# Moving the FP8 rounding of 24 tiles from the end of the attention to its middle, in a decoder block on one Trainium2 core

## The reference

```python
x = x + attention(layernorm(x))          # 32 query heads, 8 KV heads of 64, RoPE, causal, batches of 512 tokens
x = x + cross(layernorm(x), ctx)         # x, ctx: (4, 512, 512) float32
x = x + moe(layernorm(x))                # 8 experts, top 1, capacity 256, and a shared expert; hidden 704

def cross(x, weight):                    # "quantized" to float8_e4m3 and back
    xq = qdq(x, blocks of 1 x 128)       # safe = max(amax, 1e-4); round(x * 448/safe) to fp8; * safe/448
    wq = qdq(weight, blocks of 128x128)  # the same with one amax per 128 x 128 block, least 1e-6
    return einsum('emk,enk->emn', xq, wq)
```

## Time and profile before

| what | value |
| --- | --- |
| median of 3 runs | 1612.63 us (1609.43 to 1612.71) |
| the profiled execution: its own time | 1614.8 us |
| the profiled execution: its span, first to last instruction | 1613.0 us |
| mean granted TensorE clock in it | 0.956 of full speed |
| busy in the span: PE, DVE, ACT, POOL | 1467.1, 1237.6, 917.9, 1058.6 us |

### The profile page before, as it was taken

One profiled execution on the slowest core, in us unless ns is written; L12 is line 12 of the kernel. 1 busy time (PEld: TensorE's weight loads), 2 busy tenths in 40 slices (PEclk: granted clock), 3 DMA queues, 4 the chain that ended last, 5 costly groups with the idle time before them and its releaser, 6 DMA issues.

```text
span 1613.0 us, 26858 instructions
## 1 busy us (share of the span) xinstructions
PE 1467.1 (91%) x8616; PEld 1290.2 (80%) x8616; DVE 1237.6 (77%) x2986; ACT 917.9 (57%) x2277; POOL 1058.6 (66%) x1040
## 2 busy tenths in 40 slices
PE   5899999999989999999999967728889898899997
PEld 4688888888878888888888856627778787899996
DVE  6787787788887787788787879858797964677785
ACT  2587777777667777777777655422121213566562
POOL 1798888888776888888888767626252522444545
PEclk9899999999999999999999988969989899899998
DMA  5322232222312222232322333031101003577767
GB/s 189 87 73 66 81 76 71 77 81 55 81 50 63 75 74 66 81 89 55 82 76 59 112 119 92 8 125 41 52 27 53 7 27 113 160 234 221 226 209 239
DMA packets 78796, 152.13 MB, mean 94 GB/s; under 512 B 15366, under 2 KB 15622, under 8 KB 78656
## 3 DMA queue, kind: packets, MB, share of 16 engines
q1 hardware_dynamic: 76096, 142.16, 30.3%
q0 software_dynamic: 2560, 8.25, 1.5%
HBM read 87.58 MB, written 16.78 MB: 65 GB/s over the span
## 4 chain that ended last, share of the span: by engine, by line
PE 74%; DVE 12%; issue 6%; POOL 4%; ACT 2%; DMA 1%; SPq 1%; DVEq 0%; POOLq 0%; ACTq 0%
PE bank L400 15%; PE bank L401 15%; PE bank L402 15%; PE bank L442 7%; PE bank L418 5%; PE bank L457 5%; PE bank L458 5%; PE bank L419 4%; PE bank L392 2%; DVE work L943 1%; POOL P L1390 1%; DVE work L1056 1%; DVE aam L1095 1%; PE bank L429 1%; DVE st L938 1%
## 5 line engine op out<-in xcount | busy, mean ns | idle before, releaser
L742 ACT ACTIVATE P<-P,mn 128x512 f32<-128x512 f32 (+3 forms) x512 | 284.5, 556 | 221.6 <-DVE mn L994 220.9
L1390 POOL TENSOR_TENSOR P<-P,ri 128x128 f32<-128x128 f32 (+3 forms) x512 | 353.9, 724 | 10.4 <-DVE ri L983 10.4
L994 DVE CUSTOM_DVE_ANT_0 P<-bank,mask 128x512 f32<-128x512 f32 (+3 forms) x512 | 235.6, 479 | 118.3 <-PE bank L419 117.9
L1035 DVE TENSOR_TENSOR PTl<-bank,PTh 128x512 fp32r<-128x512 f32 (+1 forms) x384 | 229.2, 598 | 37.0 <-ACT PTh L754 33.9
L442 PE MATMUL bank<-ident,P 128*128 128x128 f32 x1280 | 203.4, 274 | 7.2 <-POOL P L1390 7.2
L754 ACT ACTIVATE PTh<-bank 128x512 fp32r<-128x512 f32 (+1 forms) x384 | 197.6, 516 | 6.0 <-PE bank L442 2.9
L418 PE MATMUL bank<-KT,QT 128*128 128x256 f32 (+2 forms) x512 | 191.2, 373 | 7.4 <-DVE mn L994 7.3
L457 PE MATMUL bank<-PTh,VS 128*128 128x256 f32 (+2 forms) x512 | 164.5, 332 | 11.5 <-DVE PTl L1035 8.8
L400 PE MATMUL bank<-XT,Wh 128*128 128x512 f32 x384 | 165.4, 431 | 9.6 <-DVE qcs L1007 4.7
L419 PE MATMUL bank<-KT,QT 128*128 128x256 f32 (+2 forms) x512 | 167.3, 327 | 0.0
L1428 POOL TENSOR_TENSOR OTl<-Opair,OTh 128x512 fp32r<-128x512 f32 x64 | 83.5, 1305 | 120.8 <-ACT OTh L764 120.5
(11 more groups left out here) (190 smaller groups left out, 4214.5 us busy)
## 6 DMA issues: line engine op xcount, KB each, us to landing
RW<-in_wf SPq DMA_DIRECT2D x170, 256.0 KB, 3.2
QT<-qh SPq DMA_DIRECT2D x256, 64.0 KB, 2.0
QT<-ql SPq DMA_DIRECT2D x256, 64.0 KB, 2.0
Wraw<-in_wqkv SPq DMA_DIRECT2D x16, 768.0 KB, 4.8
Oraw<-in_wo SPq DMA_DIRECT2D x16, 512.0 KB, 3.4
KT<-KT SPq DMA_DIRECT2D x32, 256.0 KB, 2.9
work<-in_ctx SPq DMA_DIRECT2D x32, 256.0 KB, 2.7
krot<-kvs SPq DMA_DIRECT2D x64, 64.0 KB, 2.0
```

The costliest lines, as they stand in the source:

```text
L742: e.activation(pq, pq, ACT.Exp, bias=mn[:, z, qb:qb + 1], scale=-1.0, accum_out=rs[:, z, qb:qb + 1]).then_inc(a_exp, 1)
L994: e.tensor_tensor_reduce(P[:, z, off[qb]:off[qb] + k], bank[n % 2][:, 0:k], mask[:, 512 - k:512], -0.125, BIG, ALU.add, ALU.min, mn[:, z, ...
L1035: e.tensor_tensor(pt_part(PTl, part), bank[2 + part][:, 0:128 * n].rearrange("p (m n) -> p m n", n=128), pt_part(PTh, part).bitcast(F32), ...
L1390: e.tensor_tensor(pq, pq, ri[:, z, qb:qb + 1].to_broadcast([128, n]), ALU.mult).then_inc(g_norm, 1)
```

## The change

Of the 32 tiles 24 are now rounded in the middle of the attention: the 16 context tiles and the 8 tiles of X that belong to batches 0 and 1. The rounded tiles are written to a new tensor `kept` in DRAM, and are loaded from there when the cross attention needs them. The buffers are `xnx` (two tiles, used otherwise for the first norms) and a new `Zb` (two tiles) for the steps.

* The 16 context tiles are loaded in steps -4 to 17 for their maxima (steps 3 to 18 on DVE). One all-reduce over all 16 tiles, in step 20, takes the place of four. The context tiles are loaded again for the rounding.
* `background()` gives the step in which each of the 24 roundings begins: 22, 25, ... 46 for tiles 0 to 8 and 61, 64, ... 103 for tiles 9 to 23. In that step SP loads the tile (or, for a tile of X, DVE makes it with its scales: `tile_scales`); one step later ACT scales it (`scaled`, four instructions of 128 columns); two steps later DVE makes the steps (`steps_of`, two instructions) and POOL adds, subtracts and scales back (`background_rounded`, three instructions, the last of them with the scale broadcast over the whole tile); four steps later SP stores it (`keep`).
* The statistics of the tiles of batches 0 and 1 are taken in steps 72 to 79.
* The zeroing of the dispatch tensor (16 transfers) moves from steps 116 to 123 to steps -3 to 4, from the new `Zb`.
* At the end of the attention the context tiles and the tiles of X of batches 0 and 1 are only loaded (`load_cw`, `load_t1`) and transposed. Batches 2 and 3 of X are rounded where they were, by the same `rounded`.

```diff
@@ slots @@
         for i in range(TB):
-            plan(s - 13 + i if b else s - 3 + i // 2, "stats2", b, i)
+            if b >= 2:
+                plan(s - 13 + i, "stats2", b, i)
+                plan(s - 1 + i, "cross_round", b, i)
             plan(s + 1 + i, "cross_turn", b, i)
             plan(s + 2 + i, "cross_product", b, i)
-            plan(s - 1 + i, "cross_round", b, i)
...
-            plan(s + i // 2, "context_max", b, i)
-        plan(s + 2, "context_all", b)
-        plan(s + 3, "context_scales", b)
-        for i in range(TB):
-            at = s + 4 + i + i // 3
-            plan(at, "context_round", b, i)
-            plan(at + 2, "context_turn", b, i)
+            plan(s + 6 + i + i // 3, "context_turn", b, i)
...
+def background():
+    return [22 + 3 * j if j < 9 else 34 + 3 * j for j in range(NBG)]
@@ scalar_engine @@
+            def scaled(j):
+                y = xnx[:, j % 2, :]
+                if j < NCTX:
+                    need.wait_ge(v_cscale, 1)
+                    need.wait_ge(d_by[j % 2], 16 * (j // 2 + 9))
+                else:
+                    need.wait_ge(v_bscale, j - NCTX + 1)
+                for c in range(4):
+                    k = wsc[:, 1, 4 * j + c:4 * j + c + 1] if j < NCTX else asc[:, j % 4, 0, c:c + 1]
+                    last = e.activation(y[:, tokens(c)], y[:, tokens(c)], ACT.Copy, scale=k)
+                last.then_inc(a_scaled, 1)
...
                     pair(h - 3)
+                if h - 1 in begins:
+                    scaled(begins[h - 1])
@@ vector_engine @@
                 if t >= 2 * TB:
                     need.wait_ge(p_xt, t - 1)
+                    need.wait_ge(d_keep, 16 * 9)
...
+            def tile_scales(j):
+                t = j - NCTX
+                y = xnx[:, j % 2, :]
+                need.wait_ge(d_keep, 16 * (j - 1))
+                after()
+                chain(normed(y, t))
+                after()
+                chain(e.tensor_reduce(aam[:, j % 4, :], four(y), AX.X, ALU.max, apply_absolute_value=True))
+                after()
+                scales(aam[:, j % 4, :], asc[:, j % 4, 0, :], asc[:, j % 4, 1, :], 1e-4).then_inc(v_bscale, 1)
+
+            def steps_of(j):
+                y, q = xnx[:, j % 2, :], Zb[:, j % 2, :]
+                need.wait_ge(a_scaled, j + 1)
...
+                chain(e.tensor_scalar(q.bitcast(U32), y.bitcast(U32), 0x7F800000, None, ALU.bitwise_and))
+                after()
+                e.tensor_scalar(q, q, 2.0 ** -6, 1.5 * 2.0 ** 20, ALU.max, ALU.mult).then_inc(v_bq, 1)
...
                     rotate(unit, 1, 1)
+                if 3 <= h < 3 + NCTX:
+                    context_max(h - 3)
+                if h == 21:
+                    context_scales()
+                if 72 <= h < 72 + 2 * TB:
+                    need.wait_ge(v_x, last_x(h - 72) + 1)
+                    stats_of(h - 72)
+                if h == 72 + 2 * TB - 1:
+                    rstd_of(slice(0, 2 * TB))
+                if begins.get(h, 0) >= NCTX:
+                    tile_scales(begins[h])
+                if h - 2 in begins:
+                    steps_of(begins[h - 2])
...
                 if 0 <= h < NH:
                     masked(h, 0)
@@ gpsimd_engine @@
+            def background_rounded(j):
+                y, q = xnx[:, j % 2, :], Zb[:, j % 2, :]
+                need.wait_ge(v_bq, j + 1)
+                e.tensor_tensor(y, y, q, ALU.add).then_inc(g_badd, 1)
+                need.wait_ge(g_badd, j + 1)
+                e.tensor_tensor(y, y, q, ALU.subtract).then_inc(g_bq, 1)
+                need.wait_ge(g_bq, j + 1)
+                d = wsc[:, 0, 4 * j:4 * j + 4] if j < NCTX else asc[:, j % 4, 1, :]
+                e.tensor_tensor(four(y), four(y), d.unsqueeze(2).to_broadcast([128, 4, 128]), ALU.mult).then_inc(g_kept, 1)
...
                     rotate(unit)
+                if h == 20:
+                    need.wait_ge(v_cmax, NCTX)
+                    e.partition_all_reduce(wsc[:, 0, :], wam[:, :, :].rearrange("p i c -> p (i c)"), 128,
+                                           bass.bass_isa.ReduceOp.max).then_inc(g_call, 1)
+                if h - 2 in begins:
+                    background_rounded(begins[h - 2])
@@ sync_engine @@
+            def keep(j):
+                need.wait_ge(g_kept, j + 1)
+                if j >= 1:
+                    need.wait_ge(d_keep, 16 * j)
+                e.dma_start(keptv[j], xnx[:, j % 2, :]).then_inc(d_keep, 16)
...
+            def load_t1(t):
+                need.wait_ge(d_keep, 16 * NBG)
+                if t < 3:
+                    need.wait_ge(p_kv, NU)
+                else:
+                    need.wait_ge(p_turn, turn_at["cross_turn", (t - 3) // TB, (t - 3) % TB] + 1)
+                e.dma_start(T1[t % 3], keptv[NCTX + t]).then_inc(d_t1[t % 3], 16)
...
+                if h in (-4, -3):
+                    load_background(h + 4)
+                if 3 < h < 2 + NCTX:
+                    load_background(h - 2)
+                if h - 4 in begins:
+                    keep(begins[h - 4])
+                if begins.get(h, NCTX) < NCTX:
+                    load_background(NCTX + begins[h])
```

More of the change, by code:

```diff
@@ L15 @@
 CHUNK_BANK = (4, 5, 7)
+NCTX, NBG = 16, 24
 class Once:
@@ L173, in decoder @@
         xd = nc.dram_tensor("xd", (NE * CAP, D), F32).ap()
+        kept = nc.dram_tensor("kept", (NBG * 128, D), F32).ap()
         oe = nc.dram_tensor("oe", (NE * CAP, D), F32).ap()
@@ L183, in decoder @@
         d_cw = [sem(f"d_cw{i}") for i in range(3)]
+        d_t1 = [sem(f"d_t1{i}") for i in range(3)]
+        d_by = [sem(f"d_by{i}") for i in range(2)]
+        d_keep = sem("d_keep")
         d_xe = [sem(f"d_xe{i}") for i in range(2)]
@@ L214, in decoder @@
         NCT = 4
-        rounds = [x for x in in_order if x[0] in ("context_round", "cross_round")]
+        rounds = [x for x in in_order if x[0] == "cross_round"]
+        begins = {at: j for j, at in enumerate(background())}
         round_at = {x: n for n, x in enumerate(rounds)}
@@ L524, in turn @@
                     need.wait_ge(v_turn, n - 1)
+                t = b * TB + i
                 if stage == "context_turn":
-                    need.wait_ge(g_q, round_at["context_round", b, i] + 1)
+                    need.wait_ge(d_cw[t % 3], 16 * (t // 3 + 1))
+                elif stage == "cross_turn" and b < 2:
+                    need.wait_ge(d_t1[t % 3], 16 * (t // 3 + 1))
                 elif stage == "cross_turn":
@@ L1631, in side_slot @@
                     stage, b, i = x
-                    if stage == "context_max":
-                        load_cw(b, *((3, 0) if i == 0 else (i - 1, 1)))
-                    elif stage == "context_turn":
-                        if i == 0:
-                            load_cw(b, 3, 1)
-                        elif b + 1 < NB:
-                            load_cw(b + 1, i - 1, 0)
+                    t = b * TB + i
+                    if stage == "context_turn" and t + 3 < NCTX:
+                        load_cw(t + 3)
+                    elif stage == "cross_turn" and t + 3 < 2 * TB:
+                        load_t1(t + 3)
                     elif stage == "load_x":
@@ L1676, in sync_engine @@
                     side_slot(h - NH - 15)
-                if h == NH - 14:
-                    for i in range(3):
-                        load_cw(0, i, 0)
-                if NH - 12 <= h < NH - 4:
+                if h in (-4, -3):
[6 more added lines that the diff above has]
+                    load_background(NCTX + begins[h])
+                if -3 <= h < 5:
                     for i in range(2):
                         need.wait_ge(g_zero, 1)
-                        e.dma_start(xdz[2 * (h - NH + 12) + i], T1[0]).then_inc(d_zero, 16)
+                        e.dma_start(xdz[2 * (h + 3) + i], Zb[:, 0, :]).then_inc(d_zero, 16)
+                if h == NH - 14:
+                    for t in range(3):
+                        load_cw(t)
+                if h == NH - 8:
+                    for t in range(3):
+                        load_t1(t)
                 if h == NH - 6:
```

97 lines of the change are left out of this document (42 added, 55 removed).

## The result

The changed kernel takes 1657.83 us (median of 4 runs, 1653.38 to 1665.72) against 1612.04 before: ratio 1.029, 95% interval 1.025 to 1.033. The forecast was 1596, faster than before, its range 1562 to 1624. The profiled execution took 1658.05 us with a span of 1656.2, 43.2 more than before.

The account below looks back on a forecast made before the run. The prediction took PE to bound the kernel except where the attention ends and the MoE begins. From a 1613.0 us span, minus 66 saved plus 50 of costs gave 1597, a median of about 1596 us, likeliest range 1582 to 1608.

Parts of the forecast that it names:

- The two sums: Whole kernel: 66 us saved at the attention's end and behind it, 50 us of costs added, mostly in the attention.
- The tail: Steps 120 to 134 and behind the attention: removed roundings, all-reduces and waits save 66 us.
- The all-reduce: Step 20, on POOL ahead of head 20's `normalised`: PE stalls for 10 us, plus 4 for the clock, 14.
- POOL: In the attention: three instructions per tile, 3.7 us, delay `normalised` and stall PE by 18 us over 72 heads.
- the slack of that is the end of POOL's four instructions to PE's L442: In the attention: room before POOL's lateness stalls PE's transposes, 0.9 to 6.3 us over eight heads.
- PE waiting for L1390's successor: In the attention: PE should wait for this POOL output ahead of the transposes of heads 0, 4 and 6 of eight.
- DVE: In the attention: inserted instructions exceed a 1.7 us slack, 12 us, plus 6 for `tile_scales`; 15 of the 18 counted.
- the 3 us for maxima and statistics: Maxima in steps 3 to 18 and statistics in 72 to 79 fit into DVE's free time and cost 3 us.
- The third rival: In the attention: DVE and POOL block each other, 1.4 us per fast DVE instruction, giving 1621 us; chance 0.14.
- The last rival: In the attention: POOL becomes the bound and its 3.7 us blocks stall PE in full, giving 1653 us; chance 0.11.
- The signs: Eight heads take about 62 us (64 in steps 82 to 105); wrong below 60, above 66, or steps 120 to 134 over 100.
- The clock: After the all-reduce's stall in step 20: a lower granted clock for PE adds 4 us.

Follow-up runs that it names:

- e7: Changed kernel with only the 16 context tiles rounded in the attention, X rounded where the kernel before does it: 1634.72 us, ratio 1.014 to the kernel before.
- e4: Changed kernel with the all-reduce in step 20 replaced by setting the scales' inputs to 1: 1647.13 us, ratio 1.021 to the kernel before.
- e1: Changed kernel with POOL's three rounding instructions per tile working on 4 columns instead of 512: 1628.63 us, ratio 1.009 to the kernel before.
- e9: Changed kernel with POOL's three instructions of a tile spread one per step over three successive steps, same work: 1645.60 us, ratio 1.019 to the kernel before.
- e13: Changed kernel with each inserted DVE TENSOR_SCALAR replaced by a copying TENSOR_REDUCE, so nothing is rounded: 1636.23 us, ratio 1.014 to the kernel before.
- e14: Changed kernel with inserted TENSOR_SCALARs replaced by TENSOR_REDUCE copies and POOL's three instructions spread one per step: 1620.46 us, ratio 1.005 to the kernel before.
- e12: Changed kernel with only the context tiles rounded in the attention and POOL's instructions spread one per step: 1625.82 us, ratio 1.008 to the kernel before.
- after: The changed kernel itself, with nothing further altered: 1657.83 us, ratio 1.029 to the kernel before.

## Why the prediction was wrong, step by step

- **The two sums.** The forecast had 66 off the tail and 50 onto the attention; the runs show 70.7 and 113.9. The forecast priced a tile at (18 + 15)/24 = 1.4 us of PE. e7, which has no tiles of X in the attention, splits it: 16 tiles of context cost 28.8 + 17.5 + 1.9 = 48 us, 3.0 each; the eight of X, the rest of steps 82 to 106, cost 41.5 - 1.9 = 40, 5.0 each; the statistics 24.9 - 17.5 = 7.4; the maxima 6.3 (steps 3 to 19); the all-reduce 11.6. So a tile costs 3.6 on the average, above the 2.0 from which on the forecast itself expected a slower kernel.
- **The tail** (66): right in sum, 70.7. From step 120 to the last addition it gave 30.6 (69.7 to 48.7 us, and 57.1 to 47.5), forecast 40. Before the MoE's first products it gave 13.1, as forecast. What lies behind gave 26 instead of 13: the stretch after those products has 46.6 us of PE in 48.3 where it had 37.3 in 48.3.
- **The all-reduce** (14): right in size, 11.6 in step 22, 10.7 in e4's time. The road was another: through `ql` and DVE, not through `normalised`.
- **POOL** (18): 29 by e1, in which DVE also waits less at the port. One step that failed is "the slack of that is the end of POOL's four instructions to PE's L442". It looked at one of POOL's users. The narrow one is on DVE: `rotate`, which waits for `ql` and passes POOL's lateness into DVE's queue. e9 shows it: with 1.3 us at a time the 8 us of waits for `ql` go and steps 23 to 51 cost 13 us less. The forecast's sign of this, PE waiting for L1390's successor, did not appear: 0.8 us.
- **DVE** (15): this is the term that was mis-sized most. Of the 88 us of the 24 tiles e1 takes off 29; what is left, some 59 us by difference, is DVE's part (an estimate, since e1 shortens DVE's waits too), and the 3 us for maxima and statistics were 14. Two things were wrong. The slack was taken from the last low part to the weighing, 1.7 us with the wait. But `attn_out` stands between them; its row for the place of the earlier trace rows, in the kernel before, is

```profile
584.30 0.69 DVE L1044 TENSOR_TENSOR X<-X,bank 128x512 f32<-128x512 f32 x1
```

  and ends at 584.99, 0.60 us before the weighing at 585.59. Over steps 24 to 106 that gap has a median of 0.56 before and is at its floor of 0.15 to 0.2 in 10 steps of 83 before and 41 after. So what DVE does ahead of masked(h, 0) is nearly all paid by PE. The other is the price of an instruction. The mean of L1119 and L1121 is 0.95 and 0.91 us, which the forecast had (1.0). But of the small instructions of `tile_scales`, taken together at 0.8, one (L1077) has a median of 0.98 where 0.17 is its best. The step 2.1 - 1.7 was also written as 0.5 where it is 0.4; that is 2 us in all.
- **The third rival** (DVE and POOL block each other, 1621) was nearest in mechanism: e13 takes 21.6 us off. The Trainium skill, "SBUF — State Buffer", "Who interferes with whom", says that `tensor_reduce` never contends on trn2 and `tensor_scalar` can; the rows above agree: none of the 48 copies is stretched, and the TENSOR_SCALARs are. The rival's price failed in that it came with the too wide slack, and left out the small instructions and several POOL instructions in a row; its 1.4 us for each fast instruction was above the 0.95 and 0.91 measured.
- **The last rival** gave 1653, near the time, but that is by chance, as its mechanism is refuted: POOL has 32 of 241 us free, PE does not wait for it, and POOL's part is worth 29 us (e1), not 89.
- **The signs.** Eight heads were to take 62 to 64 us, and above 66 was named as wrong; they take 66.5 in steps 23 to 51 and 71.6 in 82 to 106. Steps 120 to 134 take 96, under the 100 named.
- **The clock** had a place among the costs only at the all-reduce. In two stretches of the attention that were at 1.00, it is 0.98 and 0.96: 241 x 0.02 + 224 x 0.04 = some 14 us, an estimate from the granted clock, which fell where PE had waited. Two waits and what came after them, PE in steps 85 and 86 of the changed kernel:

```profile
757.48 0.47 PE L464 MATMUL bank<-PTh,VS 128*128 128x512 f32 x1
...
765.59 0.44 PE L425 MATMUL bank<-KT,QT 128*128 128x384 f32 x1 [1.76 <-DVE mn L1020]
...
768.13 0.77 PE L464 MATMUL bank<-PTh,VS 128*128 128x512 f32 x1 [1.22 <-DVE X L1070]
```

  The same product takes 0.77 instead of 0.47 us. The granted clock is 1.00 from 757.4 to 758.7 us and 0.50, the level of 1.2 GHz, from 768.1 to 771.0.

By cause, the 114 us split as far as the runs show them: about 11 the all-reduce, 21 the port beyond what the somewhat longer copies cost, 16 to 18 the size of POOL's blocks. With all three away (e14 without its all-reduce) some 63 would be left. In e14 that is mostly 24 tiles of 1.4 us on DVE and for eight of them 2 us more, the maxima and the statistics, with almost no slack under them; that this is paid one for one was argued from the 0.15 to 0.6 us, and not separated by a run from ACT's share.

No version that does the whole work beat the kernel before. e12 shows why: with 16 tiles the attention costs 54 us more, 11.5 of them for the all-reduce, and the tail gives 47.

## What to carry to other kernels

Before work is put "beside" a full engine, list every user of each engine's output, also the buffers and banks that it frees, and take the smallest slack; lateness travels through in-order queues, and here moving the work mostly changed which wait showed it. Beside a busy POOL, look at the spread of each DVE instruction's length, and not at its best: a TENSOR_SCALAR of four columns waited here through six POOL instructions in a row (6.02 us), while TENSOR_REDUCE kept its length. Splitting POOL's work (12 us) and the form that does not wait (21.6 us) were the two levers that helped; making an instruction tiny does not take its wait away. PE, 100% busy at the full clock before, lost twice here: by the waits, and by the lower clock after them.

## What the runs showed of the hardware

- DVE's TENSOR_SCALAR of 128x4 took 0.17 us alone, 2.07 beside one POOL instruction of 2.35, and 6.02 beside six in a row. TENSOR_REDUCE from SBUF (665 to 687 ns), and TENSOR_TENSOR with a PSUM operand (677 to 691), kept their length in the same surroundings. TENSOR_TENSOR with both operands in SBUF did not: L999, 11 times in `after`, took 0.68 at best, 0.89 in the median and 1.70 at most.
- The all-reduce cost POOL the same in the middle of its elementwise work as in the tail: 5.61 us before, 0.54 itself, 6.89 after it.
- ACT's four copies of 128 columns, 0.39 us each, took 1.27 us together, and four of one column, 0.28 each, still 0.84.
